# Graph network kernel: four turned tiles of the matrix are read raw again and turned by VectorE in the passes

## What is computed

```
h = relu(layernorm(x));  x = x + layer(h)         (four times)
layer 0:  e = h + weights(h);   adj @ (adj.T @ e), then layernorm, + h
layer 1:  adj @ h
layer 2:  T1 = adj @ h;  T2 = 2 adj @ T1 - h;  T3 = 2 adj @ T2 - T1;  out = h W0 + T1 W1 + T2 W2 + T3 W3 + b
layer 3:  relu(D (adj + I) D (h W + b)),  D = diag(rowsum(adj) + 1)^-0.5
```

## Time and profile before

| | us |
|---|---|
| three runs: median (lowest to highest) | 1448.79 (1447.44 to 1451.46) |
| profiled execution: its own time | 1448.4 |
| its span, first to last instruction | 1446.2 |
| outside the span | 2.2 |
| TensorE busy | 1419.2 (98%) |
| VectorE busy | 491.8 (34%) |
| ScalarE busy | 399.3 (28%) |
| bytes moved by DMA | 523.26 MB, 362 GB/s on average |

### The profile page before, as it was taken

The page is one execution under the profiler, slowest core; times in us unless marked ns, Lnnn a source line. Parts: engine busy times, 40 slices in busy tenths (PEclk is TensorE's granted clock), DMA queues, the critical chain, the costliest instruction groups (busy, mean ns, idle before and its releaser), DMA issues.

```text
span 1446.2 us, 18473 instructions
## 1 busy us (share of the span) xinstructions
PE 1419.2 (98%) x7601; PEld 600.5 (42%) x7601; DVE 491.8 (34%) x1082; ACT 399.3 (28%) x885; POOL 84.4 (6%) x67
## 2 busy tenths in 40 slices
PE   6999999999999999999999999999999999999998
PEld 3555555555555563333333333333333333333332
DVE  6694544544546533331132211011311121101044
ACT  2378778677776551000000000000000000000000
POOL 2210000000000038000000000000000000000000
PEclk9999999999999999999999999999999999999999
DMA  9999999999999998999996797899797948996998
GB/s 322 382 422 409 419 414 413 419 410 411 412 402 371 391 420 341 420 421 420 421 409 215 320 363 295 320 352 323 302 336 263 312 179 357 392 377 227 356 419 316
DMA packets 97607, 523.26 MB, mean 362 GB/s; under 512 B 18764, under 2 KB 18804, under 8 KB 54644
## 3 DMA queue, kind: packets, MB, share of 16 engines
q1 hardware_dynamic: 90436, 520.40, 91.4%
q10 hardware_dynamic: 7088, 1.67, 0.5%
HBM read 415.88 MB, written 106.17 MB: 361 GB/s over the span
## 4 chain that ended last, share of the span: by engine, by line
PE 78%; DMA 16%; ACT 3%; DVE 2%; POOL 1%; issue 1%; SPq 0%; ACTq 0%; POOLq 0%; DVEq 0%
PE turned L640 33%; PE acc L640 29%; DMA raw<-in_adj_dram 13%; PE t_acc L651 8%; PE turned L673 5%; ACT staged L882 3%; DMA over_wide<-adj_t 2%; PE turned L828 1%; DMA w_in<-in_L_gnn_W_i_dram 0%; PE t_rows L812 0%; PE turned L834 0%; DVE staged L1174 0%; PE acc L703 0%; ACT over_last L882 0%; PE t_acc L802 0%
## 5 line engine op out<-in xcount | busy, mean ns | idle before, releaser
L1134 DVE STREAM_TRANSPOSE staged<-raw 32x256 f32<-32x256 f32 x448 | 195.1, 435 | 5.8
L651 PE MATMUL t_acc<-raw,E 128*64 128x384 f32 (+1 forms) x1120 | 185.3, 478 | 5.1 <-DMA raw<-in_adj_dram 5.0
L882 ACT ACTIVATE staged<-turned 128x512 f32<-128x512 f32 x303 | 152.7, 636 | 104.1 <-PE turned L673 103.7
L926 ACT ACTIVATE t_t<-raw 128x768 uint8<-128x768 f32 (+1 forms) x216 | 177.2, 901 | 0.0
L640 PE MATMUL acc<-staged,t_cur 128*64 128x512 f32 x720 | 161.1, 596 | 0.0
L673 PE MATMUL turned<-ident,raw 128*128 128x128 f32 x1376 | 159.5, 274 | 0.0
L673 PEld LDWEIGHTS turned<-ident,raw 128*128 128x128 f32 x1376 | 149.8, 140 | 21.7 <-issue 21.7
L640 PE MATMUL turned<-over_last,C 128*64 128x512 f32 x672 | 152.1, 592 | 0.0
L651 PEld LDWEIGHTS t_acc<-raw,E 128*64 128x64 f32 x1120 | 78.4, 138 | 109.3 <-issue 85.7
L1277 POOL TENSOR_TENSOR rstd<-rstd,minus_half 128x8 f32<-128x8 f32 (+1 forms) x30 | 44.2, 1475 | 1265.9 <-DVE rstd L1036 1265.9
L640 PE MATMUL turned<-over_last,R 128*64 128x512 f32 x512 | 116.5, 593 | 0.0
(11 more groups left out here) (139 smaller groups left out, 1061.9 us busy)
## 6 DMA issues: line engine op xcount, KB each, us to landing
over_last<-adj_t SPq DMA_DIRECT2D x181, 1024.0 KB, 9.1
staged<-adj_t SPq DMA_DIRECT2D x91, 1024.0 KB, 9.4
raw<-in_adj_dram SPq DMA_DIRECT2D x60, 1536.0 KB, 19.5
adj_t<-staged SPq DMA_DIRECT2D x30, 3072.0 KB, 18.0
over_wide<-adj_t SPq DMA_DIRECT2D x23, 1024.0 KB, 7.7
raw<-in_adj_dram SPq DMA_DIRECT2D x10, 1024.0 KB, 15.0
adj_t<-over_last SPq DMA_DIRECT2D x8, 1024.0 KB, 14.9
adj_t<-C SPq DMA_DIRECT2D x2, 1024.0 KB, 21.7
```

Of the source, the lines that this page charges most:

```text
L651: last = nc.tensor.matmul(t_acc[h * D:(h + 1) * D, 0:columns], E[:, m * SUB + a, :], raw_of(g, m)[:, a, h * columns:(h + 1) * columns], st ...
L882: nc.scalar.activation(turned_into(g, u)[:, i * B:(i + 1) * B], turned[n % TURN_BANKS][:, :], ACT.Copy) \
L926: nc.scalar.activation(passed[n % 2][:, 0:chunks(g) * P], raw_of(g, m)[:, a, :], ACT.Copy, accum_out=deg_part[:, m * SUB + a, g:g + 1]).th ...
L1134: last = nc.vector.transpose(dst[b * SQ:(b + 1) * SQ, :, :, q * SQ:(q + 1) * SQ], src[q * SQ:(q + 1) * SQ, :, :, c * P + b * SQ:c * P + (b ...
```

## The change

Four tiles, one each of groups 1 to 4: (m, k) = (4, 5), (3, 8), (2, 11) and (3, 14), the last third of the columns of their pair and group, are not written to `adj_t`: the four stores are 2 MB in place of 3 MB and wait for the copies of the first 8 banks only. In the passes these tiles are needed 12 times. Each time SP loads the raw blocks into slot 0 (`room_raw`, over `over_wide`) with four DMAs of 256 KB in 512-byte pieces, ahead of an ordinary load that the planner picks, and VectorE turns them into the tile's slot of the ring in four quarters, each of four transposes of 32 partitions x 512 elements, placed at the end of chosen steps. The last quarter raises `room_turned`, on which TensorE waits instead of a DMA, and SP before it loads the next raw tile. Slot 0 serves ordinary tiles only up to step 27; from then to the end of the kernel the ring has 14 slots in place of 15. `BUSY_BEHIND` lists the steps behind a row's end in which no quarter may stand.

```diff
+UNSTORED = [(4, 5), (3, 8), (2, 11), (3, 14)]
+QUARTERS = 4
+BUSY_BEHIND = [(1, 2, 3, 4, 7, 8, 9), (1, 2, 3), (1, 2, 3), (1, 2, 3, 4, 6), (1, 2)]
+ROOM_LANDS, ROOM_AHEAD = 6, 8
+ROOM_FROM = 28
...
+        last_raw = max(n for n in range(len(self.tiles)) if n not in self.slot and self.tiles[n][1:3] in UNSTORED)
         for n in range(len(self.tiles)):
             if n not in self.slot:
-                place = min(empty, key=lambda x: x[0])
+                no_room = n > last_raw or n in self.step_tile and self.step_tile.index(n) < ROOM_FROM
+                place = min((x for x in empty if no_room or x[1] != 0), key=lambda x: x[0])
                 empty.remove(place)
...
+                if self.tiles[n][1:3] in UNSTORED:
+                    self.turned_no[n] = len(self.turned_no) + 1
+                else:
...
+    def place_turning(self):
...
+        for n in self.turned_no:
+            free = step_of[self.slot_before[n]][-1]
+            asked = max(end + 1, free - ROOM_AHEAD, step_of[self.room_after][-1] + 1)
+            after = next(x for x in self.loads if self.slot_before[x] is not None and step_of[self.slot_before[x]][-1] >= asked)
+            self.rooms_before.setdefault(after, []).append(n)
+            s = max(free + 1, end + 1)
+            while sum(products[asked:s]) < ROOM_LANDS:
+                s += 1
+            for q in range(QUARTERS):
+                while s in row_ends:
+                    s += 1
+                self.quarters_in.setdefault(s, []).append((n, q))
+                end = s
+                s += 1
+            assert end < step_of[n][0], (self.tiles[n], end, step_of[n])
...
         def wait_loaded(eng, n):
-            if n in plan.load_no:
+            if n in plan.turned_no:
+                eng.wait_ge(room_turned, plan.turned_no[n])
+            elif n in plan.load_no:
                 eng.wait_ge(whole_in[plan.slot[n]], 16 * plan.load_no[n])
...
             def store(g, m):
-                wait_copied(sp, g, m)
-                at = g * CHUNKS * PAIR
-                sp.dma_start(adj_t[m, :, at:at + STAGE_WORDS], staged_pair(g, m)).then_inc(stored_by(g, 2 * m)[0], 16)
+                at, words = g * CHUNKS * PAIR, STAGE_WORDS
+                if (m, (g + 1) * CHUNKS // 2 - 1) in UNSTORED:
+                    words = STAGE_WORDS - TILE_WORDS
+                    sp.wait_ge(chunk_copied, COPIED_NO[g, m, words // B - 1])
...
+                else:
+                    wait_copied(sp, g, m)
+                sp.dma_start(adj_t[m, :, at:at + words], staged_pair(g, m)[:, 0:words]).then_inc(stored_by(g, 2 * m)[0], 16)
...
+            def load_room(n):
+                p, m, k, dual = plan.tiles[n]
+                if plan.turned_no[n] > 1:
+                    sp.wait_ge(room_turned, plan.turned_no[n] - 1)
+                else:
+                    sp.wait_ge(multiplied, plan.used_no(plan.room_after))
+                for c in range(2):
+                    for h in range(2):
+                        at = (2 * c + h) * SUB
+                        sp.dma_start(room_raw[:, at:at + SUB, :],
+                                     pair_v[:, m, h, :, (2 * k + c) * P:(2 * k + c + 1) * P]).then_inc(room_in, 16)
...
             for n in plan.loads[len(AT_START):]:
+                for x in plan.rooms_before.get(n, []):
+                    load_room(x)
                 sp.wait_ge(multiplied, plan.used_no(plan.slot_before[n]))
                 load_turned(n)
...
+            def turn_room(n, q):
+                if q == 0:
+                    dve.wait_ge(room_in, 64 * plan.turned_no[n])
+                    dve.wait_ge(multiplied, plan.used_no(plan.slot_before[n]))
+                tile = whole[plan.slot[n]].rearrange("p (b n) -> p b n", n=P)
+                for b in range(4):
+                    last = nc.vector.transpose(tile[b * SQ:(b + 1) * SQ, :, q * SQ:(q + 1) * SQ],
+                                               room_raw[q * SQ:(q + 1) * SQ, :, b * SQ:(b + 1) * SQ])
+                if q == QUARTERS - 1:
+                    last.then_inc(room_turned, 1)
...
             for s in range(N_STEPS):
...
+                for n, q in plan.quarters_in.get(s, []):
+                    turn_room(n, q)
```

More of the change, by code:

```diff
@@ L69 @@
 EARLY_FROM, EARLY_EVERY, EARLY_ROWS = 2, 2, 2
+UNSTORED = [(4, 5), (3, 8), (2, 11), (3, 14)]
+ROOM_BLOCKS = 2 * CH
+QUARTERS = 4
+BUSY_BEHIND = [(1, 2, 3, 4, 7, 8, 9), (1, 2, 3), (1, 2, 3), (1, 2, 3, 4, 6), (1, 2)]
+ROOM_LANDS, ROOM_AHEAD = 6, 8
+ROOM_FROM = 28
 def kept_slot(m, j):
@@ L200, in __init__ @@
         loads_of = {}
+        self.turned_no = {}
+        last_raw = max(n for n in range(len(self.tiles)) if n not in self.slot and self.tiles[n][1:3] in UNSTORED)
         for n in range(len(self.tiles)):
             if n not in self.slot:
-                place = min(empty, key=lambda x: x[0])
+                no_room = n > last_raw or n in self.step_tile and self.step_tile.index(n) < ROOM_FROM
+                place = min((x for x in empty if no_room or x[1] != 0), key=lambda x: x[0])
                 empty.remove(place)
@@ L205, in __init__ @@
                 _, j, self.slot_before[n] = place
-                loads_of[j] = loads_of.get(j, 0) + 1
-                self.slot[n], self.load_no[n] = j, loads_of[j]
-                self.loads.append(n)
+                self.slot[n] = j
+                if self.tiles[n][1:3] in UNSTORED:
+                    self.turned_no[n] = len(self.turned_no) + 1
+                else:
+                    loads_of[j] = loads_of.get(j, 0) + 1
+                    self.load_no[n] = loads_of[j]
+                    self.loads.append(n)
@@ L209, in __init__ @@
+                if j == 0 and n < last_raw:
+                    self.room_after = n
                 if j != ONCE:
                     empty.append((self.used_no(n), j, n))
+                if n == last_raw:
+                    empty = [x for x in empty if x[1] != 0] + [(self.used_no(n), 0, n)]
+        self.place_turning()
+    def place_turning(self):
+        step_of = {}
+        for s, n in enumerate(self.step_tile):
+            for x in [n] * (n is not None) + self.duals_in.get(s, []):
+                step_of.setdefault(x, []).append(s)
+        products = [(n is not None) + len(self.duals_in.get(s, [])) for s, n in enumerate(self.step_tile)]
+        row_ends = {s + i for s, r in self.ended.items() for i in BUSY_BEHIND[self.rows[r][0]]}
+        self.rooms_before, self.quarters_in, end = {}, {}, 0
+        for n in self.turned_no:
[13 more added lines that the diff above has]
+            assert end < step_of[n][0], (self.tiles[n], end, step_of[n])
@@ L298, in gnn_stack @@
         whole = [w[:, :] for w in over_wide + over_last] + over_staged + over_c12 + [over_y]
+        room_raw = over_wide[0][:, :].rearrange("p (b k) -> p b k", k=P)
         out_rows = sq
@@ L323, in gnn_stack @@
         weights_ready = sem("weights_ready")
+        room_in = sem("room_in")
+        room_turned = sem("room_turned")
         x_in = [sem(f"x_in{i}") for i in range(len(X_PARTS))]
@@ L373, in gnn_stack @@
         adj_v = adj_d.rearrange("(m a p) k -> p m a k", a=SUB, p=P)
+        pair_v = adj_d.rearrange("(m a h p) k -> p m h a k", a=SUB, h=2, p=P)
         x_v = x_d.rearrange("(t p) d -> p t d", p=P)
@@ L567, in store @@
             def store(g, m):
-                wait_copied(sp, g, m)
-                at = g * CHUNKS * PAIR
-                sp.dma_start(adj_t[m, :, at:at + STAGE_WORDS], staged_pair(g, m)).then_inc(stored_by(g, 2 * m)[0], 16)
+                at, words = g * CHUNKS * PAIR, STAGE_WORDS
+                if (m, (g + 1) * CHUNKS // 2 - 1) in UNSTORED:
+                    words = STAGE_WORDS - TILE_WORDS
+                    sp.wait_ge(chunk_copied, COPIED_NO[g, m, words // B - 1])
+                    if (g, m, MOVED_BANK) in MOVED_NO:
+                        sp.wait_ge(bank_moved, MOVED_NO[g, m, MOVED_BANK])
+                else:
+                    wait_copied(sp, g, m)
+                sp.dma_start(adj_t[m, :, at:at + words], staged_pair(g, m)[:, 0:words]).then_inc(stored_by(g, 2 * m)[0], 16)
             def store_kept(u):
```

## The result

The changed kernel takes 1479.3 us (median of 4 runs, 1476.7 to 1480.9) against 1449.7 us for the kernel before in the same comparison: 29.7 us more, a ratio of 1.0203 with a 95% interval of 1.0187 to 1.0219. The profiled execution took 1480.9 us with a span of 1479.0; its span is 32.8 us longer than that of before.

What follows compares the result with a forecast made beforehand. DMA sets the first part's pace with TensorE 0.3 to 0.6 us a step behind; in the passes TensorE leads, with the line full early and at the end. 1448.4 - 7 + 9 + 18 = 1468.4, so 1468.5 us; range 1455 to 1481.

Steps and rivals of the forecast that it cites:

- First part, 7 us gained: First part: four stores 1 MB smaller give DMA 10.2 us back; capped by TensorE's floor, 7 us gained, ends 3 and 9.7.
- The raw load, 3.5 us, and the transpose, 0.70 us: Passes: a raw load costs 3.5 us (2.49 to 4.6), a 32 x 512 transpose 0.70 us (0.53 to 0.87).
- Pass 0 to pass 1, 3.5 + 1 + 1.5: Passes 0 and 1: losses of 3.5 us at step 39, 1 at row (0,3)'s end, 1.5 at row (1,4)'s save.
- Row (3,4), 3 us: Pass 3: quarters end at 1169.0 us, row (3,4)'s save, at 1165.06 before, waits for them; 3 us lost.
- Elsewhere, nothing: Passes: the other turns stand where the line has room, and the ring's lost slot costs nothing there.
- The end, 18 us: Last pass: raw load of (4,5), 16 transposes and row (4,3)'s delayed work hold back the last row; 18 us, from 13.3 to 23.
- Its signs: Whole kernel: 15.0 us steps, passes 7 us earlier, 192 transposes at 0.70 us, step 39 wait, row (3,4)'s save late, end wait.
- The last sign: End: TensorE waits over 8 us for VectorE before the last product, then VectorE does row (4,3) before the last row.
- That the last tile is ready in time: End: the last raw load lands by 1426.4 us, leaving first part and a little of pass 0: 1442 us; chance 0.05.
- That VectorE becomes a second line in pass 0: Pass 0: quarters block VectorE on raw loads and layer norms come late, 5 us plus 5 more: 1478 us; chance 0.14.
- That the relief doesn't come: First part: it runs by the loop turn, load, product, so steps stay at 15.3 us: 1475 us; chance 0.06.

Runs made afterwards that it cites:

- the ring of 14: Kernel before with only slot 0 taken out of the ring for tiles of step 28 and later, all tiles stored: 1452.8 us, ratio 1.0019.
- one transpose of 16: Changed kernel with 15 of each turn's 16 transposes left out, raw loads, waits, slots and order kept: 1458.9 us, ratio 1.0053 to before.
- the passes alone: Changed kernel with the full 3 MB stores and their full wait; raw loads, turns and 14-slot ring stay: 1484.8 us, ratio 1.0238 to before.
- the stores alone: Kernel before with the four stores cut to 2 MB, passes loading the neighbouring tile for each unstored one: 1445.3 against 1450.5 us, ratio 0.9971.
- the 8 KB pieces: Changed kernel with each raw load one 1 MB DMA in 8 KB pieces from the stored neighbour tile: 1473.5 us, ratio 1.0154 to before.
- without (3,8): Changed kernel with three unstored tiles, (4,5), (2,11) and (3,14), and (3,8) stored: 1463.7 us, ratio 1.0090 to before.
- the last version: Changed kernel with two unstored tiles, (3,11) and (1,17), slot 0 out of the ring from step 28 to 266: 1447.6 us, ratio 0.9979 to before.

## Why the prediction was right, and where it was off

The direction, the place and the mechanism were right, and the time lies in the range (1479.3 in 1455 to 1481), near the upper end of a range of 26 us. The expected loss was 20 us; it is 29.7: the relief was put too high, and the passes ahead of the end too low. By its own steps:

- *First part, 7 us gained.* Mis-sized: 4.2 us alone, 3.8 in the changed kernel's execution. Of the 6.4 us that the three stretches of five steps stood above 14.98 us a step, 4.7 went: they came down to 15.05, 15.04 and 15.19 us and not to the floor. The little that was taken for the last stretch didn't come either. Its waits on raw loads, 3.3 us before, are (447 to 548 us: us in total, times, longest)

```profile
PEld t_acc L723 <- DMA raw<-in_adj_dram: 5.0, 4, 1.7
```

  and it takes 101.1 us against 99.3. That isn't the edit's doing, as far as the traces tell: the ring of 14 has all its stores and takes 100.9 us there with 4.9 us of these waits, and "one transpose of 16" has the four stores cut and takes 99.3 with 3.1. A raw block can't be fetched before its buffer is turned, so a relieved line may be unable to work ahead; that fits the rate of 404 GB/s, and it wasn't tested by itself.
- *The raw load, 3.5 us, and the transpose, 0.70 us.* Right: 3.5 to 4.0 us by the packets, and 702 ns.
- *Pass 0 to pass 1, 3.5 + 1 + 1.5.* The 3.5 at step 39 is right: the passes alone lose 3.3 us up to there. The change loses 4.4, because the passes begin earlier and the line doesn't: the stores alone, without any raw load, lose 0.8 us by step 30. Row (0,3) costs 1.7, row (1,4) 2.0, and row (0,1) 1.3, which the prediction had at nothing: the quarters of (2,11) hold back that row's save, and TensorE waits for its layer norm. The three waits at row ends vanish with the turns cut short; row (0,3)'s vanishes with the 8 KB pieces too, so it needs both.
- *Row (3,4), 3 us.* Mis-sized by half: 6.2 us. The wait for the save is 3.2 us, as worked out. What was missed is that TensorE comes back from it at a lower granted clock, 0.54 in the 6 us that follow, and starts 17 matmul records there instead of 32.
- *Elsewhere, nothing.* 1.2 us between steps 228 and 321, all of it at 319 and 320; with the 8 KB pieces it is nothing.
- *The end, 18 us.* 13.6 + 5.9 = 19.5 us. Right in size and in its steps. Counted with the 11.7 us by which the product of step 228 is late, the raw load lands at 1440.9 (1438.5 was forecast), its turn ends at 1452.3 (1449.7), and the last row is saved at 1460.2 (1457.6), behind row (4,3) as said. What the prediction didn't see is why the raw load stands so late. It took the long line as enough; but the load was asked for about 20 us late, because slot 0 was still being turned, and without (3,8) over half of the end's cost goes. The clock falls here too, and costs little: the last two products take 3.37 and 3.68 us instead of 1.89 to 1.94, but what follows each of them waits for VectorE longer than that. Only the turning of the last row on TensorE is in the chain, with 1.12 us instead of 0.66.
- *Its signs.* The steps, the 192 transposes, the wait near step 39 and row (3,4)'s save behind quarters came as said. The passes begin 3.8 us earlier and not about 7. The last sign, TensorE waiting over 8 us for VectorE before the last product, is met in kind and not in size: it waits 5.7 us, as 4.4 us of the delay fall to the ordinary load behind the raw one, one product earlier.
- *Rivals.* That the last tile is ready in time: not so in the change, but so without (3,8). That VectorE becomes a second line in pass 0: in a small way, 1.3 and 1.7 us. That the relief doesn't come: half of it.

The miss of 9.7 us, then: 3.2 us are the relief, 7.7 the passes ahead of the end and 1.5 the end; these come from the two profiled executions, which lie 2.8 us further apart than the medians.

## What to carry to other kernels

Work moved to an idle engine costs its latency, not its share: VectorE had 700 us to spare, and cutting its 134 us of turns short brought 22 back. If such work goes through one buffer, look for the place where two users of it follow each other closely, and count from the moment the buffer is free. Time given back to a line helps only as far as the next bound (and perhaps only while its consumers' buffers are free, which wasn't tested); put such a saving where a wait is, as the last version did, and choose what to leave out by what comes after its uses, since the same edit with other and fewer tiles went from 30 us slower to 3 us faster.

## What was not expected of the hardware

- TensorE's clock after a short wait. TensorE waited 3.2 us with VectorE still busy; then six microseconds were granted 0.54 on average, nearly all of it the lower of its two levels, 1.2 GHz instead of 2.4. It doubles the price of the wait: 6.2 us for 3.2. The page "TensorE: Matmul & The Clock Gate" of the Trainium skill (why this matters for your kernels) warns of idle gaps between bursts of matmuls; the trace agrees.
- Issues of many pieces can take nearly as long as the line. The four DMAs of one raw load, 512 pieces each, hold SP for up to 16.25 us when the line is long; a single one of them takes from 0.38 to 9.26 us:

```profile
L674 SPq DMA_DIRECT2D over_wide<-in_adj_dram x48: 383/665/9262, 594.5 to 1445.4; - x48
```

  What this costs here wasn't measured by itself. The 8 KB pieces take away the long issues and the dearer packets together and give back 7.1 us, so it is no more than that.
